# The third layer's routed experts of a four-layer kernel, worked on tiles of rows sorted by expert

## The reference, cut to what matters

```python
logits = xf @ gate_w + gate_b                       # 8 experts
top_w, top_i = jax.lax.top_k(logits, 2)
gw = jax.nn.softmax(top_w, axis=-1)
combine = (gw[:, :, None] * one_hot(top_i, 8)).sum(axis=1)
for e in range(8):
    h = gelu(xf @ w1[e] + b1[e])                    # 128 -> 512
    out = out + combine[:, e:e + 1] * (h @ w2[e] + b2[e])
shared = gelu(xf @ ws1 + bs1) @ ws2 + bs2
x = x + tanh(g_ffn[2]) * (out + shared)
```

## Time and profile before

| | |
|---|---|
| median of 3 runs | 954.08 us (950.94 to 954.89) |
| the profiled execution, its own time | 954.71 us |
| its span | 952.9 us |
| TensorE, DVE, ACT, POOL busy | 893.4, 700.5, 639.3, 497.3 us |
| mean granted TensorE clock | 0.989 of full |

### The profile page before, as it was taken

One profiled execution on the slowest core, in us unless ns is written; L12 is line 12 of the kernel. 1 busy time (PEld: TensorE's weight loads), 2 busy tenths in 40 slices (PEclk: granted clock), 3 DMA queues, 4 the chain that ended last, 5 costly groups with the idle time before them and its releaser, 6 DMA issues.

```text
span 952.9 us, 22665 instructions
## 1 busy us (share of the span) xinstructions
PE 893.4 (94%) x8025; PEld 610.5 (64%) x8025; DVE 700.5 (74%) x2142; ACT 639.3 (67%) x1460; POOL 497.3 (52%) x627
## 2 busy tenths in 40 slices
PE   7898889999999999899987999999999999999976
PEld 3344446855799987468543366746488987878533
DVE  6897988778543278986998899887744346666897
ACT  2686757776784635798675677777697448687851
POOL 5446554876872134655366365657772525533172
PEclk9998999999999999999999999999999999999999
DMA  4433241321010010002102021111010010000000
GB/s 139 121 93 90 67 124 31 89 64 37 19 32 23 10 43 3 21 25 56 42 21 73 20 58 36 36 36 36 24 49 2 14 39 1 19 19 18 20 3 24
DMA packets 67519, 39.94 MB, mean 42 GB/s; under 512 B 8263, under 2 KB 65376, under 8 KB 67408
## 3 DMA queue, kind: packets, MB, share of 16 engines
q1 hardware_dynamic: 62608, 30.44, 12.4%
q0 software_dynamic: 2208, 6.78, 2.6%
q10 hardware_dynamic: 2592, 1.26, 0.5%
HBM read 11.12 MB, written 1.05 MB: 13 GB/s over the span
## 4 chain that ended last, share of the span: by engine, by line
PE 65%; DVE 16%; POOL 6%; issue 5%; ACT 5%; DMA 1%; SPq 1%; DVEq 0%; POOLq 0%; ACTq 0%
PE banks L1087 12%; PE banks L1078 12%; PE banks L907 8%; DVE mx L1392 7%; PE banks L1047 6%; PE banks L889 4%; PE banks L866 4%; PE banks L1057 4%; PE banks L852 3%; ACT probs L758 3%; POOL h L618 2%; PE banks L1016 2%; PE banks L845 2%; POOL rn L665 2%; PE banks L839 2%
## 5 line engine op out<-in xcount | busy, mean ns | idle before, releaser
L1392 DVE TENSOR_REDUCE mx<-banks 128x4 f32<-128x1024 f32 (+1 forms) x240 | 283.6, 1215 | 29.1 <-PE banks L866 21.5
L758 ACT ACTIVATE probs<-banks 128x512 f32<-128x512 f32 (+1 forms) x512 | 258.9, 583 | 55.0 <-PE banks L889 52.0
L811 ACT ACTIVATE probs<-banks,b_sb 128x256 f32<-128x256 f32 x288 | 117.7, 473 | 73.1 <-PE banks L1078 71.6
L907 PE MATMUL banks<-probs,v_aug 128*9 128x256 f32 (+1 forms) x2048 | 147.6, 370 | 7.3 <-ACT probs L758 6.3
L1087 PE MATMUL banks<-w_sb,probs 128*128 128x128 f32 x1152 | 140.6, 277 | 0.2 <-ACT probs L758 0.2
L1087 PEld LDWEIGHTS banks<-w_sb,probs 128*128 128x128 f32 x1152 | 134.9, 192 | 5.7 <-issue 2.5
L1078 PE MATMUL banks<-hT,w_sb 128*128 128x256 f32 x576 | 137.4, 382 | 0.1
L611 POOL TENSOR_TENSOR rstd<-veps,mhalf 128x2 f32<-128x2 f32 x64 | 46.2, 722 | 163.6 <-DVE veps L1339 163.0
L665 POOL TENSOR_TENSOR rn<-ss,mhalf 128x32 f32<-128x32 f32 x16 | 88.0, 5499 | 53.3 <-DVE ss L1185 53.0
L1078 PEld LDWEIGHTS banks<-hT,w_sb 128*128 128x128 f32 x576 | 104.4, 190 | 14.7 <-DVE xs L1264 0.8
L1264 DVE SCALAR_TENSOR_TENSOR xs<-banks,comb,xs 128x128 f32<-128x128 f32 x144 | 43.7, 344 | 86.1 <-PE banks L1087 84.9
(11 more groups left out here) (197 smaller groups left out, 1471.8 us busy)
## 6 DMA issues: line engine op xcount, KB each, us to landing
k_st<-k_parts SPq DMA_DIRECT2D x192, 64.0 KB, 2.1
q_st<-q_parts SPq DMA_DIRECT2D x186, 64.0 KB, 2.1
w_sb<-in_w POOLq DMA_DIRECT2D x16, 256.0 KB, 3.5
fc_sb<-in_fc POOLq DMA_DIRECT2D x6, 256.0 KB, 4.4
x_in<-in_x SPq DMA_DIRECT2D x8, 128.0 KB, 4.0
cT<-in_ctxT SPq DMA_DIRECT2D x8, 128.0 KB, 3.3
out_x<-xs SPq DMA_DIRECT2D x8, 128.0 KB, 1.8
q_st<-mT SPq DMA_DIRECT2D x32, 16.0 KB
```

The costliest lines, as they stand in the source:

```text
L758: nc.scalar.activation(probs[s][:, part % UNIT_RING, 2 * a:2 * a + 2, 0:n], b_bank(w, a + 1)[:, 0:2 * n].rearrange("p (j q) -> p j q", j=2 ...
L811: ins = nc.scalar.activation(hid[s][:, part % UNIT_RING, c, :], b_bank(w, half + 1)[:, j * ROWS:(j + 1) * ROWS], ACT.Gelu, bias=b1_sb[:, p ...
L907: ins = nc.tensor.matmul(c_bank(b, l, u // 4)[VW * i:VW * i + VR, g % 2, q0:ROWS], v_aug[s][:, t, 4 * g + i, :], probs[s][:, u % UNIT_RING ...
L1392: nc.vector.tensor_reduce(mx[s][:, r, :, hp0:hp0 + n], banks[:, first:first + 2, :].rearrange("p a (n k) -> p a n k", n=n), AX.X, ALU.max) ...
```

## The change

For batches in pairs (0 and 1, 2 and 3, ...), the eight routed passes over all rows are replaced; the shared pass stays for each batch, with its `hidden`, `output`, `comb_turn` and `out_bias`. The pair has 512 rows with two experts each, 1024 row uses; sorted by expert and with each expert's part rounded up to whole tiles of 128 rows, they fit into 15 tiles.

- `place`, parts 0 to 8: TensorE sums ones below and before each row (small bf16 products), DVE works out where each row use goes (`goes_to`) and which expert each tile has (`tile_of`).
- `scatter`: POOL issues 8 indirect DMAs, which write the normed rows `h` to the DRAM buffer `x_rows` by index. `fetch`: SP reads it back, four tiles a DMA, into SBUF.
- `look_up`: TensorE and POOL each read the 15 expert numbers into registers.
- `weights`: POOL copies, for each tile, 516 columns (first weights and bias) of the expert that the register names from `wall` to one of four places.
- `turn_in` (two tiles), `rows_hidden` (four products of 128 columns, four Gelu of 128), `rows_out` (four products of 128 columns, the moving weights addressed by register, and a copy out on DVE).
- `keep`: SP writes the results to `y_rows`, two tiles a DMA. `collect`: POOL issues 4 indirect DMAs a batch, which gather each row's two results. `join`: four scaled additions on DVE a batch.

The order (`TURNS_TAKEN`), the banks and the list of products on zeros are new throughout: `SCRATCH` has 39 instead of 121. Several waits of one step are issued together or in another sequence, and SP clears both `x_rows` once near the end of batch 3's first attention. The core of the diff:

```diff
+TILES = 2 * RT * 2 + EXPERTS - 1
+def chosen_steps():
+    steps = [("place", 2, part) for part in range(1, PLACE_PARTS)] + [("scatter", 2, 0)]
+    steps += [("fetch", 2, n) for n in range(-(-TILES // FETCH))]
+    steps += [("look_up", 2, 0)] + [("weights", 2, j) for j in range(AHEAD)] + [("turn_in", 2, 0), ("turn_in", 2, 1)]
...
+    for j in range(TILES):
+        steps += [("rows_hidden", 2, j)] + [("weights", 2, j + AHEAD)] * (j + AHEAD < TILES)
+        if j > 0:
+            steps += out(j - 1)
+        if j % TURNED == 1 and TURNED * (j // TURNED + 2) < TILES:
+            steps += [("turn_in", 2, j // TURNED + 2)]
...
-            for n in range(CHUNKS[l]):
-                out += [("output", l, n)] + [("comb_turn", l, 0)] * (n == 0) + [("out_bias", l, 0)] * (n == 1)
-                out += [("hidden", l, n + 2)] * (n + 2 < CHUNKS[l])
...
+            out += [("output", l, SHARED), ("comb_turn", l, 0), ("out_bias", l, 0)]
+            out += chosen_steps() * (b % 2) + [("collect", l, 0), ("join", l, 0), ("join", l, 1)]
...
-        w1_sb = sb("w1_sb", [P, EXPERTS + 1, HC, P])
-        w2_sb = sb("w2_sb", [P, EXPERTS + 1, HC, D])
-        b1_sb = sb("b1_sb", [P, EXPERTS + 1, HC])
+        wall = sb("wall", [P, EXPERTS + 1, WALL])
...
+        x_rows, y_rows = ([nc.dram_tensor(f"{what}_rows{n}", (TILES * P, D), F32, kind="Internal").ap() for n in range(2)] for what in "xy")
...
+                if step == "scatter":
+                    pool.wait_ge(rows_cleared, 32)
+                    pool.wait_ge(sems["placed"], w.at_step("placed", 1, "place", b, l, PLACE_PARTS - 1))
+                    for a, n in enumerate(both(b)):
+                        for t in range(RT):
+                            for k in range(2):
+                                pool.indirect_dma_start(x_rows[b // 2 % 2],
+                                                        bass.IndirectOffsetOnAxis(ap=goes_to[b // 2 % 2][:, RT * a + t, k:k + 1], axis=0),
+                                                        h[n][:, t, :], None).then_inc(sems[f"scattered{b // 2 % 2}"], 16)
...
+                    if part >= AHEAD:
+                        pool.wait_ge(sems["b_read"], w.at_step("b_read", 1, "rows_hidden", b, l, part - AHEAD))
+                    nc.gpsimd.tensor_copy(weights_in(b, part), wall[:, bass.ds(experts[part], 1), 0:W2_AT].rearrange("p a i -> p (a i)"))                        .then_inc(sems["weights_set"], 1)
...
+                if step == "rows_hidden":
...
+                    for c in range(HC):
+                        ins = nc.tensor.matmul(b_bank(w, 1)[:, c * P:(c + 1) * P], in_first(weights_in(b, part), c), rows_turned(b, part),
+                                               start=True, stop=True)
...
+                if step == "look_up":
+                    pe.wait_ge(sems["placed"], w.at_step("placed", 1, "place", b, l, PLACE_PARTS - 1))
+                    experts = expert_numbers(nc.tensor, b)
+                if step == "rows_out":
+                    second = wall[:, bass.ds(experts[part], 1), W2_AT:WALL].rearrange("p a i -> p (a i)")
...
+                        ins = nc.tensor.matmul(a_bank(w, 1)[:, 0:D], rows_mid(b, part)[:, c, :], second[:, c * D:(c + 1) * D],
+                                               start=c == 0, stop=c == HC - 1)
...
+                if step == "rows_out":
+                    dve.wait_ge(sems["a_full"], w.at("a_full", 1))
+                    nc.vector.tensor_copy(row_tile(b, part), a_bank(w, 1)[:, 0:D]).then_inc(sems["a_read"], 1)
+                if step == "join":
...
+                    for r in range(RT):
+                        ins = nc.vector.scalar_tensor_tensor(xs[s][:, r, :], rows_back(s)[:, r, part, :], col[s][:, 4 + part, r:r + 1],
+                                                             xs[s][:, r, :], ALU.mult, ALU.add)
```

More of the change, by code:

```diff
@@ L138 @@
[L138 to L142, removed]
@@ L157 @@
+5646555455544745445766766466664677765767766676576457776767656666767567666446576666654667767576646677
+7767467667577657564776757657767747574774677646747767547576455646766477764464667677654774467677777765
+6544677767
 """
 def schedule():
-    left = [iter([(step, b, l, part) for step, l, part in stream_steps()]) for b in range(BATCHES)]
+    left = [iter([(step, b, l, part) for step, l, part in stream_steps(b)]) for b in range(BATCHES)]
     return [next(left[int(b)]) for line in TURNS_TAKEN.split() for b in line]
@@ L171, in signals @@
     s = b % SLOTS
+    two = b // 2 % 2
     return {
+        "place": {"hot_ready": int(part == 0), "a_full": int(part == 1), "a_read": int(part == 1), "placed": int(part == PLACE_PARTS - 1)},
+        "scatter": {f"scattered{two}": 16 * 4 * RT},
+        "fetch": {f"fetched{two}_{part}": 16},
+        "look_up": {},
+        "weights": {"weights_set": 1},
+        "turn_in": {"b_full": 1, "b_read": 1},
+        "rows_hidden": {"b_full": 1, "b_read": 1},
+        "rows_out": {"a_full": 1, "a_read": 1},
+        "keep": {f"kept{two}": 16},
+        "collect": {f"collected{s}": 16 * 2 * RT},
+        "join": {"x_done": 1},
         "load_x": {},
@@ new lines, in in_bias, with expert_numbers, both @@
+        def in_bias(view, c):
+            return view[:, B1_AT + c:B1_AT + c + 1]
+        def expert_numbers(engine, b):
+            _, numbers = nc.values_load_multi_w_load_instructions(
+                tile_of[b // 2 % 2][0:1, 0:TILES], engines=[engine.engine], min_val=0, max_val=EXPERTS - 1,
+                skip_runtime_bounds_check_because="a sum of comparisons, and its least value with the last expert, are in bounds")
+            return numbers
+        def both(b):
+            return (b - b % 2) % SLOTS, (b - b % 2) % SLOTS + 1
@@ L858, in head_rows, with scores @@
                 return st[s][a * HALF:(a + 1) * HALF, hp, lo:lo + n]
-            def scores(s, l, r, keys, hp0, n):
-                for a in range(2):
-                    wait_bank("a", a + 1)
+            def scores(ready, s, l, r, keys, hp0, n):
+                wait_for(*ready, w.last_read("a", 1), w.last_read("a", 2))
                 for i in range(n):
@@ new lines, in _ @@
+                if step == "turn_in":
+                    n = min(TURNED, TILES - TURNED * part)
+                    at = TURNED * part // FETCH
+                    wait_for((f"fetched{b // 2 % 2}_{at}", w.at_step(f"fetched{b // 2 % 2}_{at}", 16, "fetch", b, l, at)), w.last_read("b", 1))
+                    for j in range(n):
+                        ins = nc.tensor.transpose(b_bank(w, 1)[:, j * P:(j + 1) * P], row_tile(b, TURNED * part + j), ident[:, :])
+                    ins.then_inc(sems["b_full"], 1)
```

412 lines of the change are left out of this document (289 added, 123 removed).

## The result

Slower, by 1.3%. The kernel after takes 965.06 us (median of 3 runs, 962.55 to 967.65) against 954.08; the ratio is 1.0132, 95% interval 1.0099 to 1.0165. I had said 894. The profiled execution has a span of 963.2 us, against 952.9.

The account below looks back on a forecast made before the run. TensorE alone was taken to bound the expert stretches. From the profiled 954.7 us: - 109 (TensorE) + 3 (clock) + 15 (POOL) + 8 (registers) + 8 (round trip) + 14 (end) = 893.7, so 894 us; own range 865 to 920.

Parts of the forecast that it names:

- What bounds the kernel: Whole kernel: TensorE busy 94% of the span; 77.5% of the expert work lies where TensorE alone is the limit.
- TensorE, removed and added: Third layer's experts: 64 routed passes (224.6 us) replaced by 60 tiles (113.4) and ranks (2), a gain of 109 us.
- The round trip: Placement, scatters, fetch, keep and collection per pair: mostly covered by other batches' attention, 8 us in all show (0 to 40).
- the end: After the last tile: more steps left for DVE, tail 92 us instead of 64; 14 us given back (0 to 28).
- Rival 2: Half of the 20 us from placement to first fetched tile is uncovered in every pair: 934 us; chance 0.19.
- Filler and clock: List of matmuls on zeros cut from 121 to 39: no gain counted, 3 us for clock lost (0 to 10).
- POOL: Weight copies at 0.65 us and indirect DMAs at 1.2 make other batches' norms and splits queue: 15 us (0 to 60).
- Rival 4: Indirect DMAs bind POOL at scatters and gathers, deciding from 2.4 us each; at 3.0 the time is 984; chance 0.15.
- Registers: Reading a pair's 15 expert numbers: one 2.0 us round trip a pair, 8 us in all; address arithmetic 0.
- rival 3: Register reading and address arithmetic stop TensorE's queue, costing 41 + 24 us instead of 8: 951 us; chance 0.07.
- ACT and DVE: Busy times of two engines: ACT falls from 639 to about 590 us with some 22 table loads; DVE near 705.
- The signs of being wrong: Indirect DMA over 2.4 us, TensorE idle beside a look-up over 5, or before a pair's first transposes over 10.

Follow-up runs that it names:

- half passes in the old order: Kernel before with its 64 routed passes done only for the first 128 rows of each batch, same order of steps: 895.27 us, ratio 0.9404.
- held without laying out the list anew: Kernel before, routed passes halved, banks by one rule, even batches waiting after their third layer for their partner's last pass: 988.55 us, ratio 1.0377.

## Why the prediction was wrong, step by step

- *What bounds the kernel.* Read rightly for the kernel as it stood, wrongly for the kernel without that load. TensorE at 99.7% says what is last now, not how far behind the next thing is. That TensorE had spare engines beside it I took as proof of gain; it was only proof that no other engine was full. In the run without routed passes none was: what came next I take to be the batches' own chains of short steps.
- *TensorE, removed and added: 109 us. This is the first step that failed.* The sum itself holds: TensorE has 120 us less work at full clock, of which 17 to 23 are the 82 fillers (0.21 us each at full clock, 0.287 as I priced them), so about 100 for my 109; a tile's product took 0.136 us of busy time a record, some of it at the lower clock, and nine in ten start 0.112 us or less behind the one before, which is my price. "Nearly all of the removed passes are on the chain, so I take the whole 109" does not: half passes in the old order brought 56 for 101, no passes 75 for 224.6. So a third of the whole came back, and 55% of the half. What a chain says is its length now, not how soon another of nearly that length is met.
- *The round trip (8) and the end (14). The second step that failed,* and with it the rest of the gain went. What I priced came out: TensorE waited 5.0 us in all before the pairs' transposes, and after the last tile stand 93 us with DVE busy 78.5 of them, where I had worked out 92 with 79. But of the hold I priced only the steps left after the last tile. By my sum that tile should have ended near 800 us; it ended at 870 (before, the last pass ended at 889). All of the miss lies ahead of it. The hold works in all pairs, at any point: 56 us by the half-pass kernel in the old order and the kernel after without POOL's additions (951.0 - 895.3), 59 by the order alone, some 9 of which are fillers, 84 where held without laying out the list anew. Rival 2 named four batches in flight, two of them waiting, but put the price on 10 us from placement to tile, and its 934 counts the 8 us of the sum twice (926). The price grows with the distance between the two partners, and in the trace of before that distance could be read: the third layers' first maxima of batches 2 and 3 are 120 us apart, those of 6 and 7 95.
- *Filler and clock: 3.* The short list alone costs 8.6 in the old order, where it makes 16 us more of lower clock. The kernel after has 44 more; with the passes left out and the long list kept it was 55 more, so it comes with the waits too.
- *POOL: 15.* Near in size: 14, in which the waits for landings are, a part of my 8 for the round trip. Queueing behind bursts is part of it: 7 us of TensorE's wait for the causal select went with the DMAs. The indirect DMA takes 0.98 us, not 1.2, the copy 0.62 for my 0.65, and the copies cost nothing. Rival 4, which decides from 2.4 us, is refuted. The Trainium skill ("SBUF — State Buffer", two separate sides) gives 3100 ns for a DMA issued from GpSimd beside a DVE copy in a 2-port mode. No indirect DMA here took over 1.13 us of POOL, though DVE was busy 73% of the span; whether DVE was in such a mode beside one, the trace doesn't say.
- *Registers: 8.* A pair's fifteen numbers come with one load an engine, 1.62 to 1.82 us, eight in all, and a product's address with one register operation of 0.05 us, hidden. From 0.2 us before each of TensorE's four loads to 1.5 us behind it TensorE idles 4.2 us in all. The trace refutes rival 3. The Trainium skill ("DMA: Bandwidth & Descriptors", latency and other measured facts) has about 600 ns as the floor of one load; these are above it, and fifteen separate ones were not needed.
- *ACT and DVE.* 586.8 and 700.8 for 590 and 705, 23 table loads for some 22.
- *The signs of being wrong.* None of the three came: they watched the indirect DMA, the look-up and the wait before a pair's first transposes, and nothing watched the hold or the worth of the cut. Two figures beside them did miss: TensorE's busy time of 817.5 against 760 to 785, and a product's 0.136 against 0.11 us.
- *Put together as measured:* 951.5 - 56 (half the work, old order) + 56 (pairs and their order, fillers and registers, less what the merged waits gave) + 14 (indirect DMAs) = 965.5. This adds up because each term is the difference of two of these runs; it is no test of the account. Against my sum it says where the 71 us are: 53 in the worth of the cut (56 for 109), 23 in pairs, order, fillers and registers (56 for 8 + 14 + 8 + 3), 1 less at POOL and 3 less at the start. The two bounds that I had given, 40 for the round trip and 28 for the end, would have held the 56; "most is covered" is where I chose wrong.

The experiments did not point to a version faster than the kernel before that computes the same. One that lets each batch place its own rows in tiles of its own would lose no time to partners, at 11 tiles instead of 7.5 a batch; it wasn't tried.

## What to carry to other kernels

Before you count a cut on the busiest engine in full, leave that work out and look: here 225 us of matmul on the critical chain were worth 75, and one such run would have set the ceiling for every rewrite of them in this order. A change that joins independent streams has a price that grows with the distance at which they ran, whatever its operations cost; read that distance from the trace first, and join only neighbours. Even they cost 14 us a pair here. And when idle time of all engines grows together, look for a dependency and not for an engine.

## What was not expected of the hardware

- Indirect DMAs of 128 rows hold GpSimd 0.94 to 1.13 us each and follow one another at 1.26; the scatters land after 2.2 us and the gathers after 2.6 (medians), a scatter at the latest after 3.3.
- 37 us of copies of 516 columns on POOL, with 62% of the span busy, cost nothing (950.6 with, 951.0 without).
- At the lower of TensorE's two clock levels (1.2 GHz) the kernel after had 108.5 us of matmul, the kernel before 19.6. It lies where TensorE waits: the granted clock is 0.78 in the last 63 us, of which TensorE is busy 43.82, and was 1.00 where it was busy throughout. The 375 more products on zeros that raised the mean clock from 0.920 to 0.976 made the kernel 24 us slower.
- The list of 121 products on zeros instead of that of 39 brought 8.6 us in the order for which it was made, and cost 12 us in the kernel after and 9 in the same order without routed passes.
